# Third dense stage of a graph network kernel: the last row tile of each block scaled by ScalarE and finished by GpSimd

## The reference, cut to what matters

```python
edge_feat = gelu((x[src] + edge_attr) @ W_pre + b_pre) * bases
y = x + segment_sum(edge_feat, dst)
h = maximum(_bn(y @ W1 + b1, g1, be1), 0.0)
h = maximum(_bn(h @ W2 + b2, g2, be2), 0.0)
x = _layernorm(x + y + h)
x = _layernorm(x + second_layer(x, src, dst, edge_type))
```

## Time and profile before

| what | us |
|---|---|
| median of three runs | 2009.98 (2009.41 to 2010.18) |
| the profiled execution, its own time | 2003.11 |
| span of the profiled execution | 2001.3 |
| third dense stage in it, first `twice` product to last `normed` | 929.9 to 1351.9 |
| busy in the whole span: TensorE, VectorE, ScalarE, GpSimd | 1774.9, 1624.2, 1304.9, 1088.0 |

### The profile page before, as it was taken

The page is one execution under the profiler, slowest core; times in us unless marked ns, Lnnn a source line. Parts: engine busy times, 40 slices in busy tenths (PEclk is TensorE's granted clock), DMA queues, the critical chain, the costliest instruction groups (busy, mean ns, idle before and its releaser), DMA issues. The chain is left out here.

```text
span 2001.3 us, 27312 instructions
## 1 busy us (share of the span) xinstructions
PE 1774.9 (89%) x8655; PEld 1386.4 (69%) x8655; DVE 1624.2 (81%) x2365; ACT 1304.9 (65%) x1818; POOL 1088.0 (54%) x1200
## 2 busy tenths in 40 slices
PE   4687489999998999999999989965999999999994
PEld 3465378888886776766666666644788888888883
DVE  4678556766767999997999999994888888888884
ACT  1434246565656898887788888871666666666663
POOL 7556456676786400000555555566876576765553
PEclk8889899999999999999999999986999999999997
DMA  9999999999996899983699999974565532322110
GB/s 344 366 348 394 364 359 346 335 342 331 340 244 141 241 348 348 325 299 124 245 378 390 385 410 390 390 286 126 161 168 146 145 89 92 92 83 75 58 43 29
DMA packets 187567, 506.47 MB, mean 253 GB/s; under 512 B 26355, under 2 KB 79505, under 8 KB 187168
## 3 DMA queue, kind: packets, MB, share of 16 engines
q1 hardware_dynamic: 129888, 379.91, 51.9%
q0 software_dynamic: 47136, 73.62, 16.3%
q10 hardware_dynamic: 10400, 51.20, 6.7%
HBM read 323.94 MB, written 236.25 MB: 280 GB/s over the span
## 5 line engine op out<-in xcount | busy, mean ns | idle before, releaser
L607 POOL DMA_INDIRECT scratch_y<-sums,k_target x196 | 312.7, 1595 | 159.9 <-issue 79.9
L1041 ACT ACTIVATE d_o<-d_u,d_free 128x256 f32<-128x256 f32 x392 | 203.1, 589 | 64.0 <-POOL d_free L1078 64.0
L1015 PEld LDWEIGHTS d_pN<-k_ident,d_r 128*128 128x128 f32 x1568 | 192.0, 193 | 52.1 <-issue 46.4
L1010 PE MATMUL d_pN<-d_y,d_free 128*128 128x512 f32 x392 | 191.9, 612 | 33.6 <-DVE d_u L1104 30.1
L1015 PE MATMUL d_pN<-k_ident,d_r 128*128 128x128 f32 x1568 | 192.7, 276 | 4.9 <-ACT d_r L1030 4.9
L818 ACT ACTIVATE d_part_h<-pT 128x1024 fp32r<-128x1024 f32 x98 | 100.5, 1027 | 139.5 <-PE pT L785 125.1
L882 DVE TENSOR_TENSOR d_part_l<-pT,d_part_h 128x1024 fp32r<-128x1024 f32 x98 | 119.9, 1224 | 85.0 <-ACT d_part_h L818 85.0
L1075 POOL TENSOR_TENSOR d_free<-d_free,k_minus_half 128x8 f32<-128x8 f32 (+1 forms) x100 | 163.7, 1637 | 0.2
L1104 DVE SCALAR_TENSOR_TENSOR d_u<-d_pN,d_free,k_base 128x256 f32<-128x256 f32 x392 | 160.9, 472 | 0.0
L252 POOL DMA_INDIRECT k_ring<-in_x,k_src x100 | 120.9, 1209 | 68.7 <-PE pT L280 40.3
L61 PE MATMUL pU<-d_part_h,k_w_h 128*128 128x512 f32 x296 | 125.5, 424 | 27.2 <-DVE d_part_l L882 14.2
(11 more groups left out here) (227 smaller groups left out, 5209.7 us busy)
## 6 DMA issues: line engine op xcount, KB each, us to landing
scratch_h<-d_h SPq DMA_DIRECT2D x159, 512.0 KB, 5.9
out<-d_o SPq DMA_DIRECT2D x97, 520.0 KB, 6.0
k_ring<-scratch_y SPq DMA_DIRECT2D x98, 512.0 KB, 7.7
d_y<-scratch_y SPq DMA_DIRECT2D x98, 512.0 KB, 7.8
scratch_y<-in_x ACTq DMA_DIRECT2D x25, 2000.0 KB, 20.7
d_h<-scratch_h SPq DMA_DIRECT2D x81, 512.0 KB, 7.1
k_ring<-scratch_h SPq DMA_DIRECT2D x78, 512.0 KB, 5.2
attr<-in_attr_t SPq DMA_DIRECT2D x25, 512.0 KB, 15.1
```

The source lines that it names most:

```text
L607: pool.indirect_dma_start(out=A["y"], out_offset=bass.IndirectOffsetOnAxis(ap=K.target[:, t:t + 1], axis=0), in_=K.sums[:, t], in_offset=N ...
L1010: pe.matmul(pN[k % 4][:, 2 * two:2 * two + 2].rearrange("p j f -> p (j f)"), twice[:], y[:, k % 4, two * 2 * F:(two + 1) * 2 * F], start=T ...
L1015: last = pe.matmul(pN[k % 4][:, j, cc * P:(cc + 1) * P], r[:, k % 4, cc, j * P:(j + 1) * P], K.ident[:], start=False, stop=j % 2 == 1 and ...
L1041: last = act.activation(o[:, k % 4, j, 0:F], u[:, k % 3, j], ACT.Identity, bias=nb[:, n, j:j + 1], scale=rs[:, n, J + j:J + j + 1])
```

## The change

ScalarE now scales the fourth row tile: `scale_last(k)` writes `u[.., 3] = pN[.., 3] * rs` without the base row. GpSimd adds the base row to it (`move_last`, a `tensor_tensor` of 128x256) and later does its final scaling (`norm_last`, a `tensor_scalar` of 128x256 with two operations). VectorE scales three row tiles, ScalarE's `normed` finishes three. `bn_stats` still reads all four, so its second instruction on `u` waits for `last_moved`. Three semaphores are new. TensorE also waits for `last_scaled` before it takes a PSUM tile again, SP's store also waits for `last_normed`, and `scale_last(k)` waits for `norm_last(k - 3)`, since `u` has three places.

```diff
--- before.py
+++ after.py
@@ -954,6 +954,7 @@
     relu_done, summed, st1_done, u_done, st2_done, o_done = (
         sem("d3_relu"), sem("d3_summed"), sem("d3_st1"), sem("d3_u_done"), sem("d3_st2"), sem("d3_o_done"))
     v_done, rs_done, nb_done, root_kept = sem("d3_v_done"), sem("d3_rs_done"), sem("d3_nb_done"), sem("d3_root")
+    last_scaled, last_moved, last_normed = sem("d3_last_scaled"), sem("d3_last_moved"), sem("d3_last_normed")
 
     def real(k):
         return 0 <= k < NB
@@ -977,6 +978,7 @@
 
         def store(k):
             sp.wait_ge(o_done, k + 1)
+            sp.wait_ge(last_normed, k + 1)
             sp.wait_ge(root_kept, k + 1)
             some = slice(S.dup if order[k] == NB - 1 else 0, P)
             sp.dma_start(out_rows(order[k])[some], o[some, k % 4].rearrange("p j f -> p (j f)")).then_inc(o_out[k % 4], 16)
@@ -1004,6 +1006,7 @@
             pe.wait_ge(y_full[k % 4], 16 * (k // 4 + 1))
             if k >= 4:
                 pe.wait_ge(u_done, k - 3)
+                pe.wait_ge(last_scaled, k - 3)
             else:
                 pe.wait_ge(second.h_done, 2 * NB - (3, 2, 0, 0)[k])
             for two in range(J // 2):
@@ -1037,15 +1040,26 @@
             act.wait_ge(u_done, k + 1)
             if k >= 4:
                 act.wait_ge(o_out[k % 4], 16 * (k // 4))
-            for j in range(J):
+            for j in range(J - 1):
                 last = act.activation(o[:, k % 4, j, 0:F], u[:, k % 3, j], ACT.Identity, bias=nb[:, n, j:j + 1],
                                       scale=rs[:, n, J + j:J + j + 1])
             last.then_inc(o_done, 1)
 
+        def scale_last(k):
+            act.wait_ge(rs_done, batches(k - 3))
+            if k >= 3:
+                act.wait_ge(last_normed, k - 2)
+            act.activation(u[:, k % 3, J - 1], pN[k % 4][:, J - 1], ACT.Identity,
+                           scale=rs[:, (k - 3) % 4, J - 1:J]).then_inc(last_scaled, 1)
+
         act.wait_ge(second.coef_ready, 1)
         for k in range(6):
             relu(k)
+        scale_last(0)
+        scale_last(1)
         for k in range(NB):
+            if k + 2 < NB:
+                scale_last(k + 2)
             normed(k)
             if k + 6 < NB:
                 relu(k + 6)
@@ -1056,6 +1070,19 @@
         second.coef_pool(pool)
         pool.memset(o[:, :, :, F:FP], 0.0).then_inc(pads_clear, 1)
         pool.wait_ge(pads_clear, 1)
+        def move_last(k):
+            pool.wait_ge(last_scaled, k + 1)
+            pool.tensor_tensor(out=u[:, k % 3, J - 1], in0=u[:, k % 3, J - 1], in1=K.base[:], op=ALU.add).then_inc(last_moved, 1)
+
+        def norm_last(k):
+            n = (k - 1) % 4
+            pool.wait_ge(nb_done, k + 1)
+            pool.wait_ge(last_moved, k + 1)
+            if k >= 4:
+                pool.wait_ge(o_out[k % 4], 16 * (k // 4))
+            pool.tensor_scalar(out=o[:, k % 4, J - 1, 0:F], in0=u[:, k % 3, J - 1], scalar1=rs[:, n, 2 * J - 1:2 * J],
+                               scalar2=nb[:, n, J - 1:J], op0=ALU.mult, op1=ALU.add).then_inc(last_normed, 1)
+
         for n in range(-3, NB - 1):
             a, b, at = n + 3, n + 1, n % 4
             now = slice(0 if real(a) else J, 2 * J if real(b) else J)
@@ -1080,32 +1107,43 @@
                     pool.wait_ge(o_out[b % 4], 16 * (b // 4))
                 pool.tensor_tensor(out=o[:, b % 4, :, F], in0=v[:, at, J:2 * J], in1=rs[:, at, J:2 * J],
                                    op=ALU.mult).then_inc(root_kept, 1)
+            if real(n + 2):
+                move_last(n + 2)
+            if real(n):
+                norm_last(n)
+        norm_last(NB - 1)
 
     @block.vector
     def _(dve):
-        def pairs(out, rows):
-
-            for p in range(J // 2):
-                last = dve.bn_stats(out[:, 2 * p:2 * p + 2].rearrange("p j s -> p (j s)"),
-                                    rows[:, 2 * p:2 * p + 2].rearrange("p j f -> p f j"))
-            return last
+        def pair(out, rows, p):
+
+            return dve.bn_stats(out[:, 2 * p:2 * p + 2].rearrange("p j s -> p (j s)"),
+                                rows[:, 2 * p:2 * p + 2].rearrange("p j f -> p f j"))
 
         def first(k):
             dve.wait_ge(summed, k + 1)
             if k >= 4:
                 dve.wait_ge(rs_done, batches(k - 7))
-            pairs(st[:, (k - 3) % 4, 0:J], pN[k % 4]).then_inc(st1_done, 1)
+            for p in range(J // 2):
+                last = pair(st[:, (k - 3) % 4, 0:J], pN[k % 4], p)
+            last.then_inc(st1_done, 1)
 
         def second(k):
             dve.wait_ge(rs_done, batches(k - 3))
             if k >= 3:
                 dve.wait_ge(o_done, k - 2)
-            for j in range(J):
+            for j in range(J - 1):
+                if j == J // 2:
+                    dve.wait_ge(last_scaled, k + 1)
                 last = dve.scalar_tensor_tensor(out=u[:, k % 3, j], in0=pN[k % 4][:, j], scalar=rs[:, (k - 3) % 4, j:j + 1],
                                                 in1=K.base[:], op0=ALU.mult, op1=ALU.add)
             last.then_inc(u_done, 1)
             dve.wait_ge(u_done, k + 1)
-            pairs(st[:, (k - 1) % 4, J:2 * J], u[:, k % 3]).then_inc(st2_done, 1)
+            for p in range(J // 2):
+                if p == J // 2 - 1:
+                    dve.wait_ge(last_moved, k + 1)
+                last = pair(st[:, (k - 1) % 4, J:2 * J], u[:, k % 3], p)
+            last.then_inc(st2_done, 1)
 
         for k in range(-3, NB - 1):
             if real(k + 3):
```

## The result

The changed kernel takes 2029.18 us (median of 4 runs, 2027.77 to 2033.32) against 2010.08 us before: a ratio of 1.0098, 95% interval 1.0078 to 1.0118, or 19 us slower. Measured again beside later experiments it was 1.0081 (1.0063 to 1.0099). The profiled execution took 2028.38 us with a span of 2026.3.

A forecast was written before the change was run, and what follows sets the result against it. VectorE was taken as the bound, transfers right behind it. The profiled 2003.11 us plus 3 (loop), 1 (stage's end) and 4 (late loads) gave about 2011; as a median, 2010 + 8 = 2018 us, range 2001 to 2040.

The forecast's parts named there:

- The loop: GpSimd's batch, `move_last` and one VectorE `bn_stats` form a chain setting the period at 4.13 us, up from 4.10: +3 us.
- M: Time of GpSimd's `move_last`, the two-input addition of the base row: between 0.37 and 0.94 us, taken as 0.75.
- N: Time of GpSimd's `norm_last`, the final scaling of the fourth row tile: between 0.37 and 0.94 us, taken as 0.65.
- that rival (0.17): GpSimd's own work sets the period, 4.35 us with `norm_last` at 0.94: +24 us, 2037 us; chance 0.17.
- The cheap rival: GpSimd's new operations are cheap, `move_last` below 0.72 us, and the change pays: about 2000 us; chance 0.22.
- nothing measurable: M between 0.68 and 0.76, N below 0.7, landings as before: 2007 to 2013 us; chance 0.22.
- The loads: On SP's queue, `h2` and `y` loads behind the later store are issued 3.5 us later, slow landings are paid: +4 us.
- The bound of 12: Upper limit for the cost of late loads: about 0.15 us for each of 81 blocks, 12 us.
- The end: Last two rounds of the stage run slower under the new chain, less a shorter `normed`: +1 us.
- The port: GpSimd's 512 columns a block beside VectorE lengthen VectorE's instructions: some +10 us, 2029 us; chance 0.04.
- TensorE's floor: TensorE works 3.75 us a block, so the period could not go below that even with VectorE at 3.71.

The follow-up runs named there:

- e3_no_move: Changed kernel without `move_last` (last row tile gets no base row), VectorE's last `bn_stats` waiting for ScalarE's scaling alone: 0.9945 of the kernel before.
- e10_store_by_batch: Kernel before the change, with the store of block m also waiting for the first result of GpSimd's batch m + 1: 1.0105 of the kernel before.
- e2_lag: Changed kernel with SP's stores one iteration later in its loop, so loads can be issued one period earlier: 1.0063 of the kernel before.
- e4_early_move: Changed kernel with `move_last` moved ahead of the shift `nb` and the column of `o` in GpSimd's order: 1.0043 of the kernel before.
- e1_tail: Changed kernel with VectorE's weight split at the stage's end waiting until GpSimd's last `norm_last` is done: 1.0071 of the kernel before.

## Why the prediction was right, and where its sizes were off

It forecast 2018 us, slower, in a range of 2001 to 2040. The measured 2029 lies in it, and the loop, the late loads and the longer end are there as forecast. But it forecast 8 us and 19 were measured: two places that it had not seen, block 52 and GpSimd's last two operations, made some 6 us each. Without them the kernel would be some 7 us slower, so the sum was good for the parts that it had. That the measured number still lies inside is owed to the width of the range.

- **The loop.** Predicted 3.38 + M with M = 0.75, 4.13 us. Measured: M 0.729, period 4.13. The links summed from rows of before held: with the measured M they make 4.11, 0.02 short. The Trainium skill (GPSIMD Engine Reference, section 3.1) gives 4497 ns for such an addition of 2048 columns, from which the prediction made an estimate of 0.73 us (0.74 when it is not rounded down); the trace agrees with 0.729, where the nearest rows had only said 0.37 to 0.94.
- **N.** Predicted 0.65, measured 0.561, between the bounds. So GpSimd was not the bound, and that rival (0.17) fell. Its 2037 us was not the sum of its parts either: 2010 + 24 + 1 + 4 are 2039. The dear row of `tensor_scalar`, 0.561 us for 128 columns, turned out to equal the time for 256: a single instruction behind an idle stretch was a bad slope.
- **The cheap rival and "nothing".** The cheap one was to decide at M = 0.72. M came out at 0.729, so the loop alone was nearly level with the old period. The rival "nothing measurable" had both of its conditions on M and N met; it fell by its third, the landings, and by the end of the stage.
- **The loads.** The chain was as described: store 3.4 us later against its batch (1114.64 against a batch at 1110.78 after, 1038.75 against 1038.30 before), TensorE's waits for `y` up from 3.1 to 35.3 us. The term was 4 us, measured 8.2 by VectorE's waits and 7.8 by the distances. The bound of 12 held, but the picture behind it did not: it spread the cost over 81 blocks, where some 2 us fell, and 6 fell in block 52, behind the weights' load, which the prediction doesn't name. It had set nothing for the half clock behind a long wait, and nothing for ScalarE: `scale_last` stands behind a `relu` that waits for `h2`, which held VectorE for 3.33 us there.
- **The end.** Here a step failed. I took +1 us, from the two rounds without `first` (measured 1.8) and a shorter `normed`, and set nothing for what VectorE does beside GpSimd's last two operations. It was 6 us more.
- **The port.** I weighed contention for the steady part alone and gave it 0.04. There it is absent: the scaling takes 472 ns before and after. At the end it is there, with GpSimd as the one that is held. The Trainium skill (SBUF — State Buffer, Who interferes with whom) has both sides: an instruction with at most one SBUF input outside the two-port modes doesn't contend, while casts in a two-port mode and instructions with two SBUF inputs do. The trace agrees: 472 ns in the one case, 2.2 and 3.8 us for an operation of 0.56 in the other, and the cast alone runs its 3200 columns in 1.83 us where the subtraction needs 3.49. The first `norm_last` starts 0.06 us ahead of the cast and is held all the same; starts so close don't tell who had the port first. I had read the rule for the instructions in the loop, and not for those behind it.
- **TensorE's floor** of 3.75 us was not one: 3.71 in e3_no_move.

Left open: whether the transfers could do more than 410 GB/s here, and why e10_store_by_batch cost more than the late loads of the changed kernel (15.9 us above its median block against 9.0). Its stores are 3.9 us later and not 3.4; whether that is enough was not tried. Of the last 6 us, 4.0 are the later issue of the last store (7.9 us behind the last batch instead of 3.9) and 1.9 the longer way from there to the next stage (7.2 instead of 5.3); whether the latter comes from two stores in a row was not tried apart.

## What to carry to other kernels

Ask of work that is handed to an idle engine not how much idle time there is, but whether the idle stretch lies in a chain: here GpSimd had 1.5 us free in every block, and using 1.3 of them closed a loop as long as the old period. Follow each output that becomes later to the queue that issues it, and count what stands behind it there: one iteration's shift of the stores on SP's queue (e2_lag) was worth 7 us of the stage, and GpSimd's order (e4_early_move) 13. Look for the place where something large shares that queue, since what was slack everywhere else may end there. And read a contention rule against the instructions that follow the loop as well as those in it.

## What the runs showed of the hardware

- GpSimd takes 0.729 us for a two-input addition of 128x256 floats and 0.561 for a `tensor_scalar` with two operations of the same size. Where VectorE's casts are kept away (e1_tail), the second stays between 551 and 582 ns beside VectorE's `bn_stats` and scalings from PSUM.
- Beside VectorE's cast from f32 to fp32r (1.88 us for 128x3200) and a subtraction with two SBUF inputs (3.57 us), GpSimd's 0.56 us operation took 2.2 and then 3.8 us (5.96 together, the longest 3.775), ending 0.2 to 0.4 us behind VectorE's instruction. VectorE's two grew only from 1.83 to 1.88 and 3.49 to 3.57. The six other kernels that leave the two side by side show the same 2.2 and 3.8 us within 0.01.
- Loads and stores of this stage reached 410 GB/s at a share of 1.03, where the kernel before showed 386 at 1.02: a share of one was not yet the most that the transfers could do.
- Behind a load of 1.6 MB on the same queue, a load of 512 KB took up to 12.2 us to land, where the median was 7.5.
- Behind 4.99 us of idleness TensorE was granted 0.50 of its clock for the next 5 us (3.78 us for four products instead of 1.98). Behind 2.70 us, in the kernel before, it kept 1.00.
